# Attention weights and a turned copy of the context come from the host, in place of TensorE transposes in the preparation stage

## What is computed

```python
q = jnp.einsum('bsd,ed->bse', x, wq)
k_new = jnp.einsum('bsd,ed->bse', x, wk)
v_new = jnp.einsum('bsd,ed->bse', x, wv)
k = jnp.concatenate([k_cache, k_new], axis=1)
v = jnp.concatenate([v_cache, v_new], axis=1)
scores = jnp.einsum('bqd,bkd->bqk', q, k) * scale
attn = jax.nn.softmax(scores, axis=-1)
out = jnp.einsum('bqk,bkd->bqd', attn, v)
return jnp.einsum('bqd,ed->bqe', out, wo)
```

## Time and profile before

| what | value |
|---|---|
| median of 3 runs | 1074.34 us (1072.41 to 1076.64) |
| the profiled execution, its own time | 1074.04 us |
| its span, first to last instruction | 1072.3 us |
| TensorE matmul busy | 800.4 us, 75% of the span |
| VectorE, ScalarE, GpSimd busy | 517.3, 517.8, 476.3 us |
| preparation stage, to the first score matmul | 0 to 106.44 us |

### The profile page before, as it was taken

One profiled execution on the slowest core, in us unless ns is written; L12 is line 12 of the kernel. 1 busy time (PEld: TensorE's weight loads), 2 busy tenths in 40 slices (PEclk: granted clock), 3 DMA queues, 4 the chain that ended last, 5 costly groups with the idle time before them and its releaser, 6 DMA issues.

```text
span 1072.3 us, 20533 instructions
## 1 busy us (share of the span) xinstructions
PE 800.4 (75%) x5262; PEld 438.2 (41%) x5263; DVE 517.3 (48%) x1531; ACT 517.8 (48%) x764; POOL 476.3 (44%) x397
## 2 busy tenths in 40 slices
PE   3999999999538995477984177777777778777770
PEld 2555455555324442233542043444444444444440
DVE  6344345555444552556884244544544535453432
ACT  2334234445436663135563065566656556655550
POOL 3420000001235774300777555666766566656560
PEclk9999999999769998697996599999999999999995
DMA  8501100000147876901111358878997878779668
GB/s 278 177 20 60 60 31 22 29 31 31 31 130 206 210 174 104 321 2 50 47 47 33 94 134 217 217 156 203 220 233 195 227 168 197 182 186 230 150 111 255
DMA packets 106088, 146.55 MB, mean 137 GB/s; under 512 B 18080, under 2 KB 59296, under 8 KB 106048
## 3 DMA queue, kind: packets, MB, share of 16 engines
q0 software_dynamic: 25760, 56.56, 26.6%
q1 hardware_dynamic: 77696, 89.30, 25.6%
q10 hardware_dynamic: 2592, 0.19, 0.2%
HBM read 103.15 MB, written 42.86 MB: 136 GB/s over the span
## 4 chain that ended last, share of the span: by engine, by line
PE 38%; DMA 18%; issue 11%; DVE 11%; DVEq 8%; ACT 5%; SPq 4%; POOL 3%; ACTq 2%; POOLq 0%
PE pst L181 31%; DMA big<-in_L_ffn_w_down_dram 8%; DMA x_rows<-mid,small 6%; DVEq L1100 3%; DMA mid<-moe_normalised_rows,small 3%; DVEq L1094 2%; PE pst L1204 2%; PE pst L453 2%; POOL moe_tokens_of_experts L934 2%; DMA big<-x_rows 1%; DVE big L1086 1%; DVE xn L284 1%; ACT big L1068 1%; DVE stats L272 1%; PE pst L893 1%
## 5 line engine op out<-in xcount | busy, mean ns | idle before, releaser
L181 PE MATMUL pst<-big,mid 128*128 (+1 forms) x1392 | 278.1, 351 | 28.7 <-DVE mid L1315 16.6
L934 POOL DMA_INDIRECT moe_tokens_of_experts<-token_no,small x80 | 83.7, 1046 | 307.0 <-DVE small L987 286.9
L1398 POOL DMA_INDIRECT x_rows<-mid,small x100 | 161.1, 1611 | 130.2 <-ACT mid L1259 66.4
L181 PEld LDWEIGHTS pst<-big,mid 128*128 128x128 f16 x1392 | 134.6, 100 | 137.7 <-issue 43.8
L1388 POOL DMA_INDIRECT mid<-moe_normalised_rows,small x106 | 113.9, 1075 | 90.3 <-DVE small L1305 29.3
L1204 PE MATMUL pst<-big,mid 128*128 x520 | 129.8, 382 | 1.4 <-ACT mid L1251 0.9
L1240 ACT ACTIVATE mid<-pst 128x1024 f16<-128x1024 f16 x102 | 103.8, 1017 | 54.2 <-PE pst L1176 47.2
L1176 PE MATMUL pst<-id,mid 128*128 128x128 f16 x816 | 64.8, 224 | 59.6 <-DMA mid<-moe_normalised_rows,small 54.2
L1315 DVE SCALAR_TENSOR_TENSOR mid<-pst,small,mid 128x192 f32<-128x192 f32 (+1 forms) x100 | 42.6, 426 | 118.4 <-ACT mid L1246 117.6
L181 PE MATMUL pst<-ctxN,mid 128*128 128x512 f16 x384 | 89.8, 392 | 3.2 <-ACT mid L577 3.2
L1176 PEld LDWEIGHTS pst<-id,mid 128*128 128x128 f16 x816 | 51.6, 100 | 94.4 <-DMA mid<-moe_normalised_rows,small 40.4
(11 more groups left out here) (197 smaller groups left out, 1163.0 us busy)
## 6 DMA issues: line engine op xcount, KB each, us to landing
big<-in_L_ffn_w_gate_dram SPq DMA_DIRECT2D x32, 384.0 KB
big<-in_L_ffn_w_up_dram SPq DMA_DIRECT2D x32, 384.0 KB
big<-in_L_ffn_wi_dram SPq DMA_DIRECT2D x16, 512.0 KB
big<-in_L_ffn_w_down_dram SPq DMA_DIRECT2D x32, 256.0 KB
big<-in_L_ffn_w_down_dram SPq DMA_DIRECT2D x64, 128.0 KB
moe_normalised_rows<-xn SPq DMA_DIRECT2D x18, 256.0 KB, 2.0
mid<-in_ctx_dram SPq DMA_DIRECT2D x16, 256.0 KB, 5.1
x_rows<-big SPq DMA_DIRECT2D x16, 256.0 KB, 8.0
```

What stands on the lines that cost most here:

```text
L181: last = nc.tensor.matmul(dst, stationary(a, c), moving(b, c), start=(k == 0), stop=(k == 3 * len(parts) - 1))
L934: nc.gpsimd.indirect_dma_start(out=self.tab_d[:, :], out_offset=bass.IndirectOffsetOnAxis(ap=self.addr[j % 2][:, k:k + 1], axis=0), in_=to ...
L1398: nc.gpsimd.indirect_dma_start(out=acc_d[p][:, :], out_offset=bass.IndirectOffsetOnAxis(ap=self.si[p], axis=0), in_=self.y[p], in_offset=N ...
```

## The change

- The host lays out the four attention weights transposed, and adds a second copy of the context, transposed, as an input of its own (`ctx_turned`: 512 rows of `d`, 2048 columns of context rows).
- The 16 weight entries leave `prep`, and the 16 context tiles of L224 with their copies leave TensorE, ScalarE and VectorE. `prep` has 33 entries, where it had 49.
- Raw weights are split in SBUF, in 16 parts of 128 x 512: the high part on ScalarE (`weight_high`), interleaved with its evictions after the entries in `wafter`; the low part on GpSimd (`weight_low`), four parts at a time: `wq` before its context tiles, `wk` after 8 of them, `wv` after 12, `wo` after all 16.
- The turned context is split in 16 parts of 128 x 512: ScalarE high (`turned_high`), VectorE low (`turned_low`), each after the eviction of `prep` entries 8 to 23.
- Of the four buffers `craw`, two now hold context row tiles and two hold turned parts. SyncE's one queue alternates between the two kinds. The loads of `wv` and `wo` and the stores of zeros take new places in it.
- The routing semaphores of the two mixtures of experts are shared: the second waits for counts that go on from 8.

```diff
         prep = [("x", i) for i in range(NT)]
-        prep += [("w", n, d) for n in "qk" for d in range(ND)]
         prep += [("proj", "q", c, b) for c in range(ND) for b in range(B)]
-        prep += [("w", "v", d) for d in range(ND)]
         prep += [("proj", "k", c, b) for c in range(ND) for b in range(B)]
-        prep += [("w", "o", d) for d in range(ND)] + [("g",)]
+        prep += [("g",)]
         prep += [("projv", t) for t in range(NT)]
+        wparts = [(n, d) for n in "qkvo" for d in range(ND)]
+        wafter = {1 + k: k for k in range(ND)}
+        wafter.update({NT + k: ND + k for k in range(2 * ND)})
+        wafter.update({NT + 3 * ND + k: 3 * ND + k for k in range(ND)})
...
                 elif j[0] == "proj":
-                    pe.wait_ge(prep_lo, at[("w", j[1], ND - 1)] + 1)
+                    pe.wait_ge(w_lo_s, ND * ("qkvo".index(j[1]) + 1))
+                    pe.wait_ge(prep_lo, NT)
...
+        def turned_high(act, k):
+            act.wait_ge(t_in_s[k % 2], 16 * (k // 2 + 1))
+            nc.scalar.activation(turned_part(k, 0), craw[2 + k % 2], ACT.Copy).then_inc(t_hi_s, 1)
+
+        def turned_low(dve, k):
+            dve.wait_ge(t_hi_s, k + 1)
+            nc.vector.tensor_tensor(turned_part(k, 1), craw[2 + k % 2], turned_part(k, 0), ALU.subtract).then_inc(t_lo_s, 1)
...
+        def weight_high(act, k):
+            act.wait_ge(w_in_s[k // ND % 2], 16 * (k // (2 * ND) + 1))
+            nc.scalar.activation(weight_part(k, 0), weight_raw(k), ACT.Copy).then_inc(w_hi_s, 1)
+
+        def weight_low(pool, n):
+            for k in range(ND * n, ND * (n + 1)):
+                pool.wait_ge(w_hi_s, k + 1)
+                nc.gpsimd.tensor_tensor(weight_part(k, 1), weight_raw(k), weight_part(k, 0), ALU.subtract).then_inc(w_lo_s, 1)
...
                 nc.scalar.activation(prep_dst(j, 0), prep_src(n), ACT.Copy).then_inc(prep_hi, 1)
-            for k in range(0, NCT, 2):
-                act.wait_ge(ctx_full, k + 1)
-                nc.scalar.activation(*ctx_move(k), ACT.Copy).then_inc(ctx_moved[0], 1)
+                if n in wafter:
+                    weight_high(act, wafter[n])
+                if NT <= n < NT + NCT:
+                    turned_high(act, n - NT)
...
+            weight_low(pool, 0)
             for k in range(NCT):
-                pool.wait_ge(c_in_s[k % 4], 16 * (k // 4 + 1))
-                nc.gpsimd.tensor_copy(ctxN[:, 0, k, :], craw[k % 4]).then_inc(ctx_hi, 1)
+                if k in (8, 12):
+                    weight_low(pool, k // 4 - 1)
+                pool.wait_ge(c_in_s[k % 2], 16 * (k // 2 + 1))
+                nc.gpsimd.tensor_copy(ctxN[:, 0, k, :], craw[k % 2]).then_inc(ctx_hi, 1)
...
+            weight_low(pool, 3)
...
             for k in range(NCT):
                 if k == 4:
+                    sp.wait_ge(w_lo_s, ND)
+                    wload(0, wv)
+                if k == 8:
                     sp.wait_ge(zero_s, 1)
                     exp0.zero_sp(sp, acc_d)
-                    sp.wait_ge(prep_full, at[("w", "q", ND - 1)] + 1)
-                    wload(0, wv)
-                    sp.wait_ge(prep_full, at[("w", "k", ND - 1)] + 1)
+                if k == 12:
+                    sp.wait_ge(w_lo_s, 2 * ND)
                     wload(1, wo)
-                if k >= 4:
-                    sp.wait_ge(ctx_lo, k - 3)
-                sp.dma_start(craw[k % 4], ct[:, k, :]).then_inc(c_in_s[k % 4], 16)
+                if k >= 2:
+                    sp.wait_ge(ctx_lo, k - 1)
+                sp.dma_start(craw[k % 2], ct[:, k, :]).then_inc(c_in_s[k % 2], 16)
+                if k >= 2:
+                    sp.wait_ge(t_lo_s, k - 1)
+                sp.dma_start(craw[2 + k % 2], ctx_turned[k % ND * P:(k % ND + 1) * P, k // ND * 512:(k // ND + 1) * 512]).then_inc(t_in_s[k % 2], 16)
```

More of the change, by code:

```diff
@@ L19, with program @@
 KEY = 65536
-def program(nc, x_in, ctx_in, mask_in, wq, wk, wv, wo, g0_in, wi0, wi1, wo0, g1_in, wg1, wu1, wd1, out):
+def program(nc, x_in, ctx_in, ctx_turned, mask_in, wq, wk, wv, wo, g0_in, wi0, wi1, wo0, g1_in, wg1, wu1, wd1, out):
     B, S, D = x_in.shape
@@ L121, in program @@
         w_in_s = [sem(f"attn_weight_loaded_{i}") for i in range(2)]
-        c_in_s = [sem(f"context_loaded_{i}") for i in range(4)]
+        c_in_s = [sem(f"context_loaded_{i}") for i in range(2)]
+        t_in_s = [sem(f"turned_context_loaded_{i}") for i in range(2)]
+        t_hi_s = sem("turned_context_high")
+        t_lo_s = sem("turned_context_low")
         g_in_s = sem("routers_and_mask_loaded")
@@ L215, in pe_prep, with turned_part, weight_part, weight_raw @@
                 last.then_inc(prep_full, 1)
[L216 to L232, removed]
+        def turned_part(k, h):
+            b = k // ND
+            return ctxT[:, h, k % ND, b * 512:(b + 1) * 512]
+        def turned_high(act, k):
[4 more added lines that the diff above has]
+            nc.vector.tensor_tensor(turned_part(k, 1), craw[2 + k % 2], turned_part(k, 0), ALU.subtract).then_inc(t_lo_s, 1)
+        def weight_part(k, h):
+            n, d = wparts[k]
+            return wT[n][:, h, d, :]
+        def weight_raw(k):
+            return wraw[k // ND % 2][:, k % ND, :]
+        def weight_high(act, k):
[5 more added lines that the diff above has]
+                nc.gpsimd.tensor_tensor(weight_part(k, 1), weight_raw(k), weight_part(k, 0), ALU.subtract).then_inc(w_lo_s, 1)
         def act_prep(act):
@@ L307, in dve_prep @@
                     norm(n + 2)
-            for k in range(1, NCT, 2):
-                dve.wait_ge(ctx_full, k + 1)
-                nc.vector.tensor_copy(*ctx_move(k)).then_inc(ctx_moved[1], 1)
+                if NT <= n < NT + NCT:
+                    turned_low(dve, n - NT)
         def pool_prep(pool):
@@ L733, in dve @@
                 self.next.place(dve, NT - 1)
+        route = {n: sem(f"routing_{t}") for n, t in (
+            ("lg_full", "logits_full"),
+            ("top_s", "largest_logit_ready"),
+            ("m_s", "choice_ready"),
+            ("pr_s", "logits_exponentiated"),
+            ("rk_full", "ranks_full"),
+            ("key_s", "keys_ready"),
+            ("addr_s", "table_rows_ready"),
+            ("sw_s", "weight_sum_inverted"),
+            ("w_s", "router_weights_ready"),
+            ("row_s", "row_normalised"),
+            ("xhi_s", "row_high"),
+            ("xlo_s", "row_low"),
+            ("nt_full", "x_transposed"),
+            ("nt_out", "x_transposed_moved"),
+        )}
         class Experts:
```

117 lines of the change are left out of this document (58 added, 59 removed).

## The result

The kernel before took 1071.98 us (median of 20 runs, 1067.72 to 1080.10), the changed kernel 1079.35 us (20 runs, 1074.58 to 1084.93). The ratio is 1.0068, with a 95% interval of 1.0051 to 1.0084: the change makes the kernel slower, by 7.4 us or 0.7%. The forecast was 1070.0 us, in a range of 1065.5 to 1075.0.

The account below looks back on a forecast made before the run. TensorE alone was taken to set the attention's start. Removals would give 13.6 us, less 3.6 for the clock and 6.0 for the wait: 4.0 gained, from 1074.04 to 1070.0 us, range 1065.5 to 1075.0.

Parts of the forecast that it names:

- What is removed (16.8 us), ends exposed: Preparation: 16.8 us of TensorE transposes go; q starts at 28.7 us, and the scores wait 1.6 us for v's last bank.
- The clock at q, 2.0 us: First projection: TensorE runs 4 us at half speed, losing 2.0 us.
- Rival 2: At q: transposes do not raise the clock, q starts as fast as before; 6.0 us gained, 1068.0 us; chance 0.13.
- The chain to wk: Before k: wk's low parts, behind queued context tiles on GpSimd, are ready at 57.4 us; TensorE stands still 6.0 us.
- rival 4: Preparation: transfers sharing engines are slower, or operations hold each other a little; 2 to 5 us more, 1072 to 1075; chance 0.18.
- rival 3: Preparation: VectorE and GpSimd hold each other up, chain to wk 9.8 us longer, 1079.8 us; chance 0.07.
- the 9 us that the prediction named as a sign of being wrong: Before k: TensorE's pause should be 5 to 7 us; under 2 or over 9 would show the prediction wrong.
- The clock after the pause, 1.6 us: Start of k: the 6 us pause lowers the clock to a mean of 0.60 over 4 us, losing 1.6 us.
- the row at 258 us: Kernel before: idle times of 1.53 and 0.64 us were followed by 4 us at mean clock 0.60, used to price the pause.
- Low parts of wv and wo, priced at nothing: GpSimd in preparation: wv's ready at about 73 us, due at 80.1; wo's at about 86, before the scores; no cost.
- The sum of the stage: Preparation: k at 57.4 us plus later terms puts the first score at 102.4 us against 106.44; 4.0 us gained.
- The rest is a rigid shift: Behind the first score, at 106.44 us before: the program is the same, so later stages only shift, without added cost.

Follow-up runs that it names:

- e4_fill: Changed kernel with 44 matmuls of 512 columns in TensorE's pause before the k projection, results unused; 1091.67 us, ratio 1.0064 to the kernel before.
- e1_wk_early: Changed kernel with the low parts of wk made ahead of GpSimd's context tile 4; 1086.79 us, ratio 1.0015 to the kernel before.
- p_dve: Changed kernel with 8 one-column memsets at the end of VectorE's first stage; 1085.44 us, ratio 1.0021 to the kernel before.
- p_pe: Changed kernel with 192 matmuls of 8 columns in TensorE's pause before k; 1091.11 us, ratio 1.0082 to the kernel before.
- b_less8: Kernel before, with unused turned context input and shared routing semaphores, VectorE's eight context tile copies given to ScalarE; 1087.70 us, ratio 1.0165.
- the last table's four kernels: Changed kernel, low parts of wk before context tile 4, wv before 8, plus 4, 8 or 16 VectorE memsets (one adds 192 matmuls); ratios 0.9909 to 0.9934.
- e8_4: Changed kernel with low parts of wk before context tile 4, of wv before tile 8, and 4 memsets on VectorE; 1059.61 us, ratio 0.9909.
- e8_16: Changed kernel with low parts of wk before context tile 4, of wv before tile 8, and 16 memsets on VectorE; 1060.62 us, ratio 0.9916.
- e2_rest: Kernel before with only the turned context as an unused input and the routing semaphores shared; 1083.78 us, ratio 0.9998.
- k1_pads: Changed kernel with 192 matmuls of 8 columns in TensorE's pause before k and 8 memsets on VectorE; 1085.86 us, ratio 1.0013.

## Why the prediction was wrong

- **What is removed (16.8 us), ends exposed.** Right. q started at 28.3 (28.7 forecast) and the last v bank showed behind v, 1.4 us.
- **The clock at q, 2.0 us.** Right: 23.04 - 20.88 = 2.2 us, with 10 matmuls in the first 4 us. Rival 2, that transposes don't raise the clock, falls with the rows of before: there q came behind 6 us of transposes without a pause and took 20.88 us, full speed from its start. By the Trainium skill's rule ("TensorE: Matmul & The Clock Gate", Part 4: PE-mode transpose) it would have been slow there too; the measurement decides.
- **The chain to wk.** Right in its links, and wrong in two sizes. The turned part was done at 35.6 (36.0). Tile 4 was issued at 39.06 (39.4), but took 8.4 us to land and not 5.5: I had given it the 5.5 us of an undisturbed `wv`, while `wv` itself now took 8.2, with a turned part ahead and others behind (rival 4). Which of these neighbours costs what is not shown. And the two subtractions did hold each other up (rival 3, in part): a cast of 0.61 us took 1.07 once, a subtraction of 1.15 took 1.66, and the four for `wk` 4.93 and not 4.4. Tile 5 was done 1.0 us later by the first two, and tile 7's load, which waits for its buffer, with it. k started at 61.56, not 57.4: 4.2 us, of which the landing has 2.5 and these operations the rest. The pause of 10.23 us is over the 9 us that the prediction named as a sign of being wrong. The Trainium skill ("GPSIMD Engine Reference", 1. Specifications) names a VectorE instruction with two inputs in SBUF beside GpSimd as contention, without a price. The rows agree, at about 0.5 us for an operation that meets one of VectorE's. Rival 3's time, 1079.8 us, lies beside the measured 1079.35 by accident: it wanted 9.8 us of such losses in the chain, and the rows have some 1.5.
- **The clock after the pause, 1.6 us.** The mechanism is shown by e4_fill, the size was 2.6: the clock stayed at 0.50 for the whole first 4 us, where the row at 258 us that I took had 0.60 after shorter idle times. That row was no firm ground either: in the changed kernel the same idle times of 1.53 and 0.65 us at 259 us were followed by a clock of 1.00 (259.2 to 263.2 us).
- **Low parts of wv and wo, priced at nothing.** Right in the changed kernel, but only since k was late: in e1_wk_early, with k on time, those of `wv` came 4.5 us late.
- **The sum of the stage.** Forecast 102.4, measured 107.62: 4.2 us of it are the chain to `wk`, 1.0 the clock after the pause. That alone would have made it 1075.2, about the top of the range and no gain.
- **"The rest is a rigid shift".** Wrong, and no rival had it. I excluded a cost because the later text is the same. Its place in VectorE's stream isn't, and at the new place the second layer's experts take 5.8 us more in the mean (3.0 in the pair that the forecast compares), with an idle time ahead of each trip's first copy that is 0.16 us longer in that pair (2.85 against 2.69). p_dve, p_pe, b_less8 and the rows of the last table's four kernels show that it is VectorE's place that does this. Why this place is bad is not shown. The Trainium skill ("Advanced Engine Details and Errata", ISA Cache) gives an engine's instruction cache lines of 256 instructions; a loop that lies across a line's edge at one place and not at the others would fit. No row here tells where an edge lies, and by a count of VectorE's instructions in the built programs there is no multiple of 256 inside the loop in either kernel, so this stays a guess.
- **What stays open.** Why the place is bad, and how the lost time reaches the end. Beside it, the kernels' second attention, from the end mark of the first experts to the first mark of the second, has two lengths that have nothing to do with the change. It took 187.1 to 189.3 us in five profiles: the two of the result and those of b_less8, e8_4 and e8_16, from the set at 1069.7 us. It took 199.5 to 203.6 us in the eleven whole-kernel profiles of the sets at 1083 to 1085 us. In all eleven the view puts waits of ScalarE and VectorE in that stretch down to "remote" (in e2_rest one of 9.4 us), in none of the five. So most of the 11 to 15 us by which these sets differ lies there, for a reason that no row names, and spans from the two groups can't be subtracted.

## What to carry to other kernels

Moving preparation from the busiest engine to the others pays only if the order of the helpers' work follows the order of the need: here two lines in GpSimd's loop decided between losing 0.7 to 0.8% and gaining 0.5%. In a queue that runs in order, price a load by what stands ahead of it and beside it, and look where the next pause opens once the first is closed. When instructions are taken out ahead of a hot loop, its place in the stream moves; if a stage with unchanged text gets slower, put a few do-nothing instructions ahead of it and look whether its time comes back.

## What I had not expected of the hardware

- Eight instructions fewer on VectorE, hundreds of us ahead of a loop, made the loop's stage 5.8 us longer in the mean. The idle time put down to issue at the head of its trips grew with it (111.0 against 102.2 us in the mean, over 39 trips).
- A 256 KB load issued right behind one of 1 MB took 8.4 us to land, against 2.5 us alone. The 1 MB took 8.2 us beside it, and 5.5 us without the loads of turned parts.
- 192 matmuls of 8 columns took 5.09 us (27 ns each) in the pause, and k was still slow behind the 4.91 us that were left of it. From k1_pads' timeline of TensorE:

```profile
52.53 5.09 PE L205 MATMUL pst<-xT,big 128*128 128x8 f16 x192
62.53 22.32 PE L183 MATMUL pst<-xT,big 128*128 128x512 f16 x96 [4.91 <-POOL big L244]
```

- The same kernel before took 1069.7 to 1085.0 us in the different sets of runs, 1.4% apart, twice the effect that was looked for. The two extremes were on the same chip, and most of the difference lies in one stretch, the second attention.
